# Six edits at the three seams of a two-layer transformer kernel: early routing weights, two moved table loads, one low part on another engine, a residual sum in PSUM

## The chip, the cores and the metric

The kernel runs on one core of a Trainium2 chip. The metric is device time in microseconds (us) of one execution, as the median of several runs. The engines are TensorE (PE, whose weight loads have their own row, PEld), VectorE (DVE), ScalarE (ACT), GpSimd (POOL) and SyncE (SP), which here only issues DMAs. They run their own instruction streams and meet through semaphores.

## The reference

An input of 8 batches x 512 tokens x 128 features passes four sublayers, each followed by a residual sum and a layernorm:

```python
x = layernorm(x + L0_attn(x))   # 16 heads of 8, softmax
x = layernorm(x + L0_ffn(x))    # 32 experts of width 64 (top 6 of 4 groups) + shared expert of width 128
x = layernorm(x + L1_attn(x))   # RMS norm, rotary, sigmoid weights divided by their sum, output projection
x = layernorm(x + L1_ffn(x))    # gated, width 384, integer weights times 1/127
```

The experts are computed densely for all tokens: each expert's hidden values are multiplied by a routing weight per token (zero for most), `combine.T` in the reference's scan, before the down product.

## The kernel before

Four stages follow each other, each a block of its own: `attention0`, `feed_forward` (called "moe" in the tile names), `attention1` and `last_stage` (tiles "ff"). At the end of a block all five engines meet at a barrier and then start the next block's streams. I call the three meeting places seams: seam 1 between `attention0` and `feed_forward`, seam 2 between `feed_forward` and `attention1`, seam 3 between `attention1` and `last_stage`. Features lie on the partitions in the feed-forward stages, and the 512 tokens of a batch are the free dimension.

**Feed-forward units.** The 32 experts are handled two at a time, with the shared expert as the last: 17 units per batch. A unit `j` has three matmuls for the gate (high and low parts of the fp32 numbers, `product`), three for the up product, and three for the down product, which PE does four steps later. ACT applies Silu to the gate in place (L1956), DVE multiplies the up product by the routing weights `cw` (`weighted_up`, L2007) and then by the gate (`weighted_hidden`, L2016), ACT rounds the hidden value to its high part `hh` (`hidden_hi`, L1966), and POOL subtracts to get the low part `hl` (`hidden_lo`, L2077). The third down matmul (L1906) waits for `hl`. PSUM has three banks each for gate and up, so that unit `j + 3` may start when the hidden value of `j` is done. The order on every engine is that of the function `step`, unrolled by hand for the first and last batches.

**Routing weights.** They are computed per batch, written to DRAM as 32 rows (`ct` to `r["weights"]`, for the first batch at L914 in the last part of `attention0`), and read back by SP, each row spread over 64 partitions, into one of eight slots of `cw` (L1862; two DMAs per unit). SP issues all reads of the first batch from the start of the `feed_forward` block.

**The first steps of `feed_forward`** also carry the end of batch 7 of the attention (`FirstOutput`): DVE divides the outputs, POOL adds the residual (L986), DVE takes the statistics, POOL computes the reciprocal root (L178 and L180) and applies the norm (L168, L171).

**The first steps of `last_stage`** carry the end of batch 7 of `attention1` (`LastOutput`, steps `k`). It uses the idle PSUM bank 7, `out_bank(1)`, called `tiles`: PE turns the outputs (k 0, L1579), DVE divides, PE turns them back (k 1, L1584), PE projects (k 2, L1589), DVE adds the bias and the residual (L1616, L1619), takes statistics (k 3), POOL the reciprocal root, DVE applies the norm in four instructions (`layernorm_apply`, L159, k 4), PE turns the result (k 5, L1595), DVE splits it into `xh` and `xl` (L1627, L1629). A unit `s` of this stage has six matmuls (L2156 to L2158 twice) and three down matmuls (L2180, L2181, L2186) three steps later; PE's step `s` calls `last.tensor` with `k = s + 1`, DVE's step `s` with `k = s`. The down product of unit 3 is the first to write bank 7 and waits for `x_parted`, which L1629 raises.

ACT loads a table when the function changes. Three tiny activations place these loads by hand: Silu at the start of `feed_forward` (L1990), Sigmoid at its end (L1993), Silu at the end of `attention1` (L1268).

## Time and profile before

| | |
|---|---|
| median of 3 runs | 1083.58 us (1083.07 to 1086.02) |
| the profiled execution | 1081.41 us, span of its instructions 1079.6 us |
| busy share of the span | PE 93%, DVE 75%, ACT 68%, POOL 43% |
| mean granted TensorE clock | 0.966 of full |
| `feed_forward` block | about 417.3 to 721.5 us |
| `attention1` block | about 721.8 to 1010.0 us |
| `last_stage` block | about 1010.3 to 1079.6 us |

Times inside the trace are us from the span's start. Since PE is busy for nearly all of the span, what matters is where it is idle, or runs at a lower clock, and which engine it then waits for. A matmul's printed duration overlaps the next one's, so a row of matmuls goes by its pitch (start to start), not by the printed durations.

### The profile page before, as it was taken

The page shows a single profiled execution, that of the slowest core. Times are in us where ns is not written, and L with a number is a line of the kernel's source. Part 1 is how long each engine was busy: PE and PEld are TensorE (multiplying, and loading weights), DVE is VectorE, ACT ScalarE, POOL GpSimd, SP SyncE. Part 2 cuts the span into 40 slices and gives each one's busy share as a digit, 9 for nine tenths or more (in the row PEclk, how much of TensorE's full clock was granted, in tenths as well). Part 3 has the DMA queues.
Part 4 walks back from the last instruction along what each step waited for, and adds up shares of the span by engine and source line. Part 5 has one row for each costly group of instructions (what it writes and reads, how often), then busy time and mean ns, then how long its engine had stood idle before and what let it go on. Part 6 is the DMA issues. An engine that isn't in the chain of part 4 may idle for free. (4 is left out here: it accounts for less than half of the span.)

```text
span 1079.6 us, 20047 instructions
## 1 busy us (share of the span) xinstructions
PE 1006.4 (93%) x5764; PEld 475.0 (44%) x5764; DVE 813.6 (75%) x1890; ACT 735.6 (68%) x952; POOL 460.3 (43%) x465
## 2 busy tenths in 40 slices
PE   3999999999999998999999999989999999999796
PEld 1122222222222244888888887753332333222485
DVE  4879999999999975887788789856555555533577
ACT  1057777777777775655555555557888898899554
POOL 0323414224143625676677676665333133300265
PEclk7569999999999999999999999989999999999998
DMA  6363122231221002334323433432522332230011
GB/s 198 108 210 105 56 76 90 62 103 54 85 89 44 2 2 97 114 111 153 116 95 109 146 114 91 155 106 83 152 75 65 94 117 81 65 88 1 1 30 49
DMA packets 74091, 97.00 MB, mean 90 GB/s; under 512 B 12716, under 2 KB 42284, under 8 KB 73644
## 3 DMA queue, kind: packets, MB, share of 16 engines
q1 hardware_dynamic: 73048, 95.17, 28.5%
q10 hardware_dynamic: 992, 1.21, 0.4%
q8 instruction: 25, 0.41, 0.2%
q14 instruction: 26, 0.21, 0.1%
HBM read 68.16 MB, written 27.79 MB: 89 GB/s over the span
## 5 line engine op out<-in xcount | busy, mean ns | idle before, releaser
L687 DVE TENSOR_REDUCE a_nmax<-a_ps_f 128x1 f32<-128x512 f32 x512 | 319.8, 682 | 27.2 <-PE a_ps_f L542 25.8
L470 ACT ACTIVATE a_prob<-a_ps_s 128x1024 f32<-128x1024 f32 x256 | 251.1, 1022 | 74.9 <-PE a_ps_s L607 73.6
L1259 ACT ACTIVATE a_prob<-a_ps_s 128x1024 f32<-128x1024 f32 x256 | 244.8, 1030 | 34.1 <-PE a_ps_s L1314 33.3
L2077 POOL TENSOR_TENSOR moe_hl<-moe_hid,moe_hh 128x512 fp32r<-128x512 f32 x136 | 176.2, 1301 | 90.8 <-ACT moe_hh L1966 90.7
L542 PE MATMUL a_ps_f<-a_ks,a_qs 48*128 48x512 bf16 x512 | 177.1, 415 | 23.9 <-DMA a_ks<-parts_k 10.1
L1956 ACT ACTIVATE moe_ps<-moe_ps 128x512 f32<-128x512 f32 x128 | 74.5, 582 | 111.8 <-PE moe_ps L1886 111.1
L620 PE MATMUL a_ps_o<-a_prob,a_va 128*32 128x512 f32 x1024 | 138.1, 612 | 0.5 <-ACT a_prob L470 0.4
L1327 PE MATMUL a_ps_o<-a_prob,a_va 128*32 128x512 f32 x1024 | 137.2, 608 | 1.0 <-ACT a_prob L1259 0.5
L542 PEld LDWEIGHTS a_ps_f<-a_ks,a_qs 48*128 48x128 bf16 x512 | 40.8, 94 | 218.8 <-DVE a_nmax L687 188.2
L607 PE MATMUL a_ps_s<-a_qs,a_ks 51*128 51x512 bf16 x512 | 135.3, 388 | 1.7 <-ACT a_prob L470 1.5
L2007 DVE TENSOR_TENSOR moe_prod<-moe_cw,moe_ps 128x512 f32<-128x512 f32 x128 | 87.3, 682 | 31.2 <-PE moe_ps L1886 28.3
L1314 PE MATMUL a_ps_s<-a_qs,a_ks 48*128 48x512 bf16 x512 | 92.8, 388 | 12.3 <-ACT a_prob L1259 9.0
L2016 DVE TENSOR_TENSOR moe_hid<-moe_prod,moe_ps 128x512 f32<-128x512 f32 x128 | 86.9, 679 | 6.9 <-DVE moe_prod L2007 1.9
L1966 ACT ACTIVATE moe_hh<-moe_hid 128x512 fp32r<-128x512 f32 x136 | 84.7, 624 | 5.2 <-DVE moe_hid L2016 5.0
L258 POOL TENSOR_TENSOR a_parts<-a_qk,g_zero 128x512 bf16<-128x512 f32 x28 | 29.2, 1044 | 137.3 <-ACT a_qk L442 66.0
L1314 PEld LDWEIGHTS a_ps_s<-a_qs,a_ks 48*128 48x128 bf16 x512 | 23.7, 93 | 133.1 <-ACT a_prob L1259 105.9
L749 POOL TENSOR_TENSOR a_msplit<-a_nmax,g_zero 128x32 bf16<-128x32 f32 x16 | 3.8, 238 | 146.6 <-DVE a_nmax L687 146.6
L1884 PE MATMUL moe_ps<-moe_xh,moe_whig 128*128 (+1 forms) x136 | 55.0, 404 | 3.4 <-DVE moe_hid L2016 3.4
L1906 PE MATMUL moe_ps<-moe_hl,moe_whid 128*128 128x512 f32 x136 | 54.0, 397 | 0.7 <-POOL moe_hl L2077 0.6
L1904 PE MATMUL moe_ps<-moe_hh,moe_wlod 128*128 128x512 f32 x136 | 53.9, 396 | 0.0
L1884 PE MATMUL moe_ps<-moe_xh,moe_whiu 128*128 (+1 forms) x136 | 53.8, 396 | 0.0
L1886 PE MATMUL moe_ps<-moe_xl,moe_whig 128*128 (+1 forms) x136 | 53.6, 394 | 0.0
(294 smaller groups left out, 1590.8 us busy)
## 6 DMA issues: line engine op xcount, KB each, us to landing
moe_cw<-r_weights SPq DMA_DIRECT2D x256, 128.0 KB, 2.9
parts_q<-a_parts SPq DMA_DIRECT2D x48, 256.0 KB, 2.5
a_qs<-parts_q SPq DMA_DIRECT2D x128, 96.0 KB, 2.4
parts_k<-a_parts SPq DMA_DIRECT2D x46, 256.0 KB, 2.5
a_ks<-parts_k SPq DMA_DIRECT2D x121, 96.0 KB, 2.5
a_xt<-in_x_t SPq DMA_DIRECT2D x8, 256.0 KB, 2.9
out_x<-g_X SPq DMA_DIRECT2D x7, 256.0 KB, 2.3
moe_wg<-in_wg SPq DMA_DIRECT2D x1, 1088.0 KB, 6.1
```

Source lines behind the costliest of these rows:

```text
L470: nc.scalar.activation(prob[:, u % PSLOTS, :, :], ps_s[:, u % 2, :, :], ACT.Exp, scale=float(P) ** -0.5).then_inc(exp_done, 1)
L542: nc.tensor.matmul(ps_f[:, bank, :], stack_rows(qs[p], h, QKR)[:, qt * P:(qt + 1) * P], stack_rows(ks[p], h, QKR), start=True, stop=True). ...
L607: mm = nc.tensor.matmul(ps_s[:, u % 2, i, :], stack_rows(ks[p], h, MXR)[:, kt * P:(kt + 1) * P], stack_rows(qs[p], h, MXR), start=True, st ...
L620: mm = nc.tensor.matmul(ps_o[j * CT:(j + 1) * CT, :], v_of_head(va[p], kt, grp * HG + j), prob[:, (2 * e + j // UN) % PSLOTS, j % UN, :], ...
L687: nc.vector.tensor_reduce(nmax[:, half_no, h % 2, col:col + 1], ps_f[:, bank, :], AX.X, ALU.max, negate=True).then_inc(max_done, 1)
L1259: nc.scalar.activation(prob[:, u % PSLOTS, :, :], ps_s[:, u % 2, :, :], ACT.Sigmoid, scale=float(HD) ** -0.5).then_inc(exp_done, 1)
L1314: mm = nc.tensor.matmul(ps_s[:, u % 2, i, :], stack_rows(ks[p], h, QKR)[:, kt * P:(kt + 1) * P], stack_rows(qs[p], h, QKR), start=True, st ...
L1327: mm = nc.tensor.matmul(ps_o[j * CT:(j + 1) * CT, :], v_of_head(va[p], kt, grp * HG + j), prob[:, (2 * e + j // UN) % PSLOTS, j % UN, :], ...
L1884: nc.tensor.matmul(dst, w[0][:, j, :], hi, start=True, stop=False)
L2007: nc.vector.tensor_tensor(prod[:, bank(j), :], cw[:, j % RC, :], ps_u[:, bank(j), :], ALU.mult).then_inc(prod_done, 1)
L2016: nc.vector.tensor_tensor(hid[:, hid_at(j), :], prod[:, bank(j), :], ps_g[:, bank(j), :], ALU.mult).then_inc(hid_done, 1)
L2077: nc.gpsimd.tensor_tensor(hl[:, part_at(j), :], hid[:, hid_at(j), :], hh[:, part_at(j), :], ALU.subtract).then_inc(hl_done, 1)
```

## The change

- **Routing weights requested earlier.** SP, at the end of its `attention0` stream, waits until the first batch's weights are in DRAM and issues the reads of units 0 to 2 (`CW_EARLY = 3`, six DMAs) there. `cw` moves to the top of the free SBUF, and slots are renumbered (`cw_slot`), so that these three units use the top three slots. In `feed_forward` SP starts with unit 3.
- **Sigmoid load moved** from after ACT's last instruction of `feed_forward` to right behind the last `hidden_hi`.
- **Silu load moved** from the end of `attention1` to the start of `last_stage`.
- **Last low part on VectorE.** For unit 16 of batch 7 DVE computes `hl` in `feed_forward`, not POOL.
- **Residual sum in PSUM.** In `LastOutput` the sum of L1619 is written to `tiles` (PSUM) and not back to `att` (SBUF), and the statistics and the four norm instructions read it there.
- **Turn later.** PE's turn of the normed tile and DVE's split of it come at k 6, not at k 5.

```diff
+RC, CW_EARLY = 8, 3
...
         sp.dma_start(self.m["r"]["weights"][0:E, :], self.m["ct"][:, :]).then_inc(self.m["c_out"], 16)
+        sp.wait_ge(self.m["c_out"], 16)
+        for j in range(CW_EARLY):
+            read_weights(sp, self.m, 2 * j, j)
...
+def cw_slot(j):
+    return (j + RC - CW_EARLY) % RC
+
+def read_weights(sp, m, row, j):
+    for i in range(2):
+        src = m["r"]["weights"][bass.ds(row + i, 1), :].broadcast_to([EI, T])
+        sp.dma_start(m["cw"][i * EI:(i + 1) * EI, cw_slot(j), :], src).then_inc(m["cw_in"][j % RC], 16)
...
             take_o(NB - 1, NO - 1)
-            nc.scalar.activation(e["table"][:, :], g["zero"][:, :], ACT.Silu)
...
-        if k == 5:
+        if k == 6:
             pe.wait_ge(self.ln["x_done"], NB)
             pe.wait_ge(self.y_taken, NB + 1)
...
-            nc.vector.tensor_tensor(att[:, :, :], att[:, :, :], self.X, ALU.add).then_inc(self.sum_done, 1)
+            nc.vector.tensor_tensor(tiles, att[:, :, :], self.X, ALU.add).then_inc(self.sum_done, 1)
         if k == 3:
             dve.wait_ge(self.sum_done, NB)
-            layernorm_stats(nc, dve, ln, NB - 1, att)
+            layernorm_stats(nc, dve, ln, NB - 1, tiles)
         if k == 4:
-            layernorm_apply(nc, dve, g, ln, NB - 1, att)
-        if k == 5:
+            layernorm_apply(nc, dve, g, ln, NB - 1, tiles)
+        if k == 6:
             dve.wait_ge(self.x_turned, NB)
...
                 def batch(b, more):
-                    for j in range(n_c):
+                    for j in range(CW_EARLY if isinstance(b, int) and b == 0 else 0, n_c):
                         load_weights(b, j)
...
-                pe.wait_ge(hl_done, n + 1 + C)
+                if isinstance(b, int) and (b, j) == (NB - 1, n_un - 1):
+                    pe.wait_ge(last_low, 1)
+                else:
+                    pe.wait_ge(hl_done, n + 1 + C)
...
                     hidden_hi(*at(b, j, HI))
+                    if head and is_last_unit(b, j):
+                        nc.scalar.activation(head.e["table"][:, :], g["zero"][:, :], ACT.Sigmoid)
...
-            if head:
-                nc.scalar.activation(head.e["table"][:, :], g["zero"][:, :], ACT.Sigmoid)
...
+                if is_last_unit(b, j):
+                    dve.wait_ge(hh_done, n_un * NB + C)
+                    nc.vector.tensor_tensor(hl[:, part_at(n_un - 1), :], hid[:, hid_at(n_un - 1), :],
+                                            hh[:, part_at(n_un - 1), :], ALU.subtract).then_inc(last_low, 1)
...
-                if at(b, j, HI) is not None:
+                if at(b, j, HI) is not None and not is_last_unit(b, j):
                     hidden_lo(*at(b, j, HI))
...
+            nc.scalar.activation(last.table[:, :], g["zero"][:, :], ACT.Silu)
             for s in steps:
                 if batch_at(s, END) is not None:
                     take_down(batch_at(s, END))
...
+            m["cw"] = nc.alloc_sbuf_tensor_at("moe_cw", [P, RC, T], F32, offset=wide - RC * T * 4)
+            m["cw_in"] = [sem(f"cw_in{i}") for i in range(RC)]
```

## Rows read from the trace of the kernel before

**Rows 1.** Windows: stretch, length, busy PE, PEld, DVE, ACT, POOL, then PEclk, DMA.
```profile
1024.00:1026.00 2.00, 2.00 (x7) 1.52 (x6) 1.38 (x2) 0.00 (x0) 0.00 (x0) 0.50 0.00 0
...
1030.00:1040.00 10.00, 10.00 (x47) 8.21 (x46) 7.55 (x29) 5.32 (x10) 7.33 (x9) 1.00 0.09 26
```

**Rows 2.** Timeline around seam 1: start, us, engine, line, tiles, idle before.
```profile
411.78 0.33 SPq L914 DMA_DIRECT2D r_weights<-moe_ct  x1
...
416.41 0.60 ACT L442 ACTIVATE moe_dsb<-a_ps_o 128x512 f32<-128x512 f32 x1 [0.52 <-PE a_ps_o L620]
417.29 10.81 SPq L1862 DMA_DIRECT2D moe_cw<-r_weights  x17
...
417.47 0.63 PE L928 MATMUL moe_ps<-g_ident,moe_dsb 128*128 128x128 f32 x4 [1.19 <-PEq L290]
...
421.29 0.69 DVE L2007 TENSOR_TENSOR moe_prod<-moe_cw,moe_ps 128x512 f32<-128x512 f32 x1 [2.17 <-DMA moe_cw<-r_weights]
...
422.79 0.63 ACT L1966 ACTIVATE moe_hh<-moe_hid 128x512 fp32r<-128x512 f32 x1 [0.62 <-DVE moe_hid L2016]
...
425.44 0.20 POOL L178 TENSOR_TENSOR a_ve<-a_mv,g_eps 128x4 f32<-128x4 f32 x1 [0.24 <-DVE a_mv L150]
...
430.29 0.19 PEld L1906 LDWEIGHTS moe_ps<-moe_hl,moe_whid 128*128 128x128 f32 x1 [0.53 <-POOL moe_hl L2077]
```

**Rows 3.** The DMA of L914, from issue to landing (source view).
```profile
DMA to landing us min/median/max: 1.6/1.6/1.6
```

**Rows 4.** Timeline around seam 2.
```profile
714.31 1.73 ACT L1966 ACTIVATE moe_hh<-moe_hid 128x512 fp32r<-128x512 f32 x3
...
715.01 3.78 POOL L2077 TENSOR_TENSOR moe_hl<-moe_hid,moe_hh 128x512 fp32r<-128x512 f32 x3 [0.78 <-ACT moe_hh L1966]
...
718.17 0.40 PE L1904 MATMUL moe_ps<-moe_hh,moe_wlod 128*128 128x512 f32 x1
...
720.00 1.28 ACT L1993 ACT_TABLE_LOAD   x1
...
720.80 0.69 DVE L2050 TENSOR_TENSOR moe_y<-moe_ps,g_X 128x512 f32<-128x512 f32 x1 [5.42 <-PE moe_ps L1916]
```

**Rows 5.** Timeline a little later: a VectorE sum beside a GpSimd one.
```profile
729.34 1.04 POOL L168 TENSOR_TENSOR moe_y<-moe_y,moe_mv 128x512 f32<-128x512 f32 x1
729.41 1.52 DVE L1416 TENSOR_TENSOR a_xr<-a_xb,a_rr 128x512 f32<-128x512 f32 x1 [1.12 <-POOL a_rr L1533]
```

**Rows 6.** Timeline around seam 3.
```profile
1007.90 0.60 ACT L1247 ACTIVATE a_osb<-a_ps_o 128x512 f32<-128x512 f32 x1 [1.25 <-PE a_ps_o L1327]
1008.52 1.28 ACT L1268 ACT_TABLE_LOAD   x1
...
1010.31 0.63 PE L1579 MATMUL ff_ps<-g_ident,a_osb 128*128 128x128 f32 x4 [2.53 <-PEq L1183]
...
1011.67 0.60 ACT L2215 ACTIVATE ff_gated<-ff_ps 128x512 f32<-128x512 f32 x1 [1.66 <-PE ff_ps L2158]
...
1012.44 0.69 DVE L2244 TENSOR_TENSOR ff_hid<-ff_gated,ff_ps 128x512 f32<-128x512 f32 x1 [0.36 <-PE ff_ps L2158]
```

**Rows 7.** Timeline of the norm of batch 7 in the last stage.
```profile
1019.77 2.49 POOL L2287 TENSOR_TENSOR ff_hl<-ff_hid,ff_hh 128x512 fp32r<-128x512 f32 x2
1019.84 3.02 DVE L159 TENSOR_SCALAR g_X<-a_att,a_mv,a_rstd 128x128 f32<-128x128 f32 x4 [0.83 <-POOL a_rstd L180]
...
1022.91 1.11 PE L1595 MATMUL ff_ps<-g_ident,g_X 128*128 128x128 f32 x4 [3.04 <-DVE g_X L159]
...
1029.39 0.47 PE L2180 MATMUL ff_ps<-ff_hh,ff_whid 128*128 128x512 f32 x1
```

**Rows 8.** Timeline: POOL's row, then DVE's, of the next norm in that stage.
```profile
1033.27 2.55 POOL L2287 TENSOR_TENSOR ff_hl<-ff_hid,ff_hh 128x512 fp32r<-128x512 f32 x2
...
1033.33 1.36 DVE L159 TENSOR_SCALAR g_X<-ff_ps,ff_mv,ff_rstd 128x128 f32<-128x128 f32 x4 [0.83 <-POOL ff_rstd L180]
```

**Rows 9.** The chain that ended last, at full clock: start, us to the next step.
```profile
1026.42 0.23 PE ff_ps L2156
...
1029.20 0.44 PE ff_ps L2193 x4
```

More of the change, by code:

```diff
@@ L1557, in attention1 @@
     return LastOutput(nc, g, w[:, 3, :], ob, osb[:, NO - 1, :], rec, att, att_t, ln, xh[:, NB - 1, :], xl[:, NB - 1, :],
-                      ot_done, rec_done, att_done, at_done, at_taken, y_done, y_taken, sum_done, x_turned, x_hi, x_parted)
+                      ot_done, rec_done, att_done, at_done, at_taken, y_done, y_taken, sum_done, x_turned, x_hi, x_parted,
+                      e["table"])
 class LastOutput:
     def __init__(self, nc, g, w, ob, osb, rec, att, att_t, ln, xh, xl, ot_done, rec_done, att_done, at_done, at_taken,
-                 y_done, y_taken, sum_done, x_turned, x_hi, x_parted):
+                 y_done, y_taken, sum_done, x_turned, x_hi, x_parted, table):
         self.nc, self.g, self.w, self.ob, self.osb, self.rec, self.att, self.att_t, self.ln = (
@@ L1570, in __init__ @@
             y_done, y_taken, sum_done, x_turned, x_hi, x_parted)
-        self.X = g["X"][:, NB - 1, :, :]
+        self.X, self.table = g["X"][:, NB - 1, :, :], table
     def tensor(self, pe, ps, k):
@@ L1764, in feed_forward @@
         RG = 3
-        RC = 8
         RH = min(4, n_un)
@@ L1780, in feed_forward @@
             ct = m["ct"]
-            cw = sb("cw", [P, RC, T])
+            cw, slot = m["cw"], cw_slot
             ps_ct = ps[0:E, 7, :]
-            c_out, cw_in = m["c_out"], [sem(f"cw_in{i}") for i in range(RC)]
+            c_out, cw_in = m["c_out"], m["cw_in"]
         g_done, u_done, silu_done, prod_done, hid_done, hh_done, hl_done, d_done, d_taken = (
@@ L1787, in feed_forward @@
         t_done, t_taken, ct_turned, ct_taken = sem("t_done"), sem("t_taken"), m["ct_turned"], m["ct_taken"]
+        last_low = sem("last_low")
         C = 6
@@ L1836, in head_at, with is_last_unit @@
             return n_un * (b - NB + 2) + j if head and isinstance(b, int) and b >= NB - 2 else None
+        def is_last_unit(b, j):
+            return isinstance(b, int) and at(b, j, HI) == (NB - 1, n_un - 1)
         def routes(b):
@@ L1859, in load_weights @@
                         sp.wait_ge(prod_done, n_un * (b - 1) + j + n_c - RC + 1 + C)
-                    for i in range(2):
-                        src = r["weights"][bass.ds(b * E + 2 * j + i, 1), :].broadcast_to([EI, T])
-                        sp.dma_start(cw[i * EI:(i + 1) * EI, j % RC, :], src).then_inc(cw_in[j % RC], 16)
+                    read_weights(sp, m, b * E + 2 * j, j)
                 def batch(b, more):
-                    for j in range(n_c):
+                    for j in range(CW_EARLY if isinstance(b, int) and b == 0 else 0, n_c):
                         load_weights(b, j)
@@ L2006, in weighted_up @@
                 dve.wait_ge(cw_in[j % RC], 32 * (n_c // RC) * b + 32 * (j // RC) + 32)
-                nc.vector.tensor_tensor(prod[:, bank(j), :], cw[:, j % RC, :], ps_u[:, bank(j), :],
+                nc.vector.tensor_tensor(prod[:, bank(j), :], cw[:, slot(j), :], ps_u[:, bank(j), :],
                                         ALU.mult).then_inc(prod_done, 1)
```

## The prediction, made before the change was run

> **What bounds the kernel now.** I read the page first: PE is busy 93% of the span, and on the chain that ended last nearly all time is PE's. So a change is worth what it takes out of PE's idle time, or out of its time at a low clock, and nothing else. The windows of the last stage show the two conditions [rows 1]: from 1030 to 1040 us PE is busy all 10 us at full clock (2.4 GHz) with DVE at 7.55 and POOL at 7.33, so there PE is the bound and an earlier start is kept to the end. From 1024 to 1026 the granted clock is 0.50 (1.2 GHz). A step of the 512-column matmuls takes 0.23 us at full clock and four turns take 0.44 [rows 9]. Then I read the timeline at the three seams and at the norm of batch 7 in the last stage, asking at each what PE waits for last. The sum is made against the profiled execution (1081.41 us, span 1079.6). The median of the runs lies 2.2 us above it, which I take as the spread of executions, so I subtract the same gain from the median.
>
> **Seam 1, early routing weights.** ACT ends the attention at 416.41 + 0.60 = 417.01 and SP's first issue of the next block is at 417.29, so the barrier costs 0.28 [rows 2]. DVE then waits 2.17 us for the first weights and starts its product at 421.29. The up product was there long before: PE starts at 417.47, and four turns (0.44) and six matmuls (1.37) with the last one's tail end by 419.5 [rows 2, 9]. What is removed is that wait. What is added is six issues on SP in front of the barrier. The first block's issues go at 10.81 / 17 = 0.636 us each. The DRAM write is issued at 411.78 and lands 1.6 us later [rows 3], so SP issues from about 413.4 and ends at 413.45 + 6 x 0.636 = 417.27. That is 0.26 after ACT: SP becomes the last at the barrier, and everybody starts 0.26 later, which costs 0.26. The DMAs themselves collide with nothing: no transfer of the attention is open then. The slots are requested from unit 3 on as before, and are needed later than before by nobody.
>
> DVE's chain gets shorter by 421.29 - 419.5 - 0.26 = 1.5, of which I lose some 0.2 to GpSimd's residual sum running beside DVE's next instruction. But PE does not get the 1.3 us. It idles three times at the start of this stage, and the last time it waits for POOL, at 430.29 [rows 2]. POOL's chain up to there starts with the first `hh`, which ACT could have begun at 422.79 - 0.62 = 422.17 (it idled 0.62 for the hidden value). In the new kernel ACT begins it as soon as it is free, at 422.17 + 0.26 = 422.43, so 0.36 earlier than before. POOL's own work follows without a gap, and its idle 0.24 before L178 goes too, since the statistics come 1.3 earlier. POOL's chain therefore gains 0.36 + 0.24 = 0.60, and PE with it. Behind 430.29 PE has no idle time worth naming. Seam 1: **-0.6**. Bounds: nothing, if POOL's work stretches by as much, to -1.3, if POOL's chain moves with DVE's.
>
> **Seam 2, low part on DVE and Sigmoid.** The last `hh` ends at 714.31 + 1.73 = 716.04, and POOL does the last three low parts one after the other until 715.01 + 3.78 = 718.79 [rows 4]. PE could have begun its last matmul one step after the one at 718.17, at 718.40; it begins at 718.85. So 0.45 us is there to gain if DVE's subtraction is ready by 718.40. DVE asks for it at about 716.1, when POOL is inside its first subtraction. Two sums over SBUF beside each other can be seen a little later [rows 5]: DVE's took 1.52 and not the 0.69 of its like in [rows 4]; it asked at 729.41, POOL's ended at 730.38, and it was done at 730.93. It waited, and then went ahead of POOL's next. If it does so here, it runs from about 716.2 to 716.9 and POOL's second subtraction ends at about 718.05, not 717.53. PE's third matmul of unit 15 waits for that, and unit 16's comes 0.80 behind (three steps and the release), at about 718.9: no gain. If POOL goes first, DVE ends at 718.2, still in time, and 0.45 is gained. I take **0**, with -0.45 and +0.3 as bounds, because in [rows 5] the one that had waited went first.
>
> The Trainium skill ("SBUF — State Buffer", section Who interferes with whom) has this as a rule: a VectorE instruction with two SBUF inputs and a GpSimd one that reads SBUF exclude each other for the whole instruction. By that rule the edit as such gains nothing or 0.45 as order decides; [rows 5] agree with it.
>
> The Sigmoid load lies at 720.00 on ACT and ends with its activation at 721.49. Moved behind the last `hh` it runs from 716.04 to 717.5, inside ACT's idle time before 719.38, so it costs nothing. It gains nothing either: DVE's sum at 720.80 + 0.69 = 721.49 ends at the same moment and holds the barrier. Without the cover it would cost what it costs now.
>
> **Seam 3, Silu.** ACT takes the last outputs until 1008.50, loads the table for 1.28 from 1008.52, runs its activation (0.2, to 1010.01), and PE starts 0.30 later, at 1010.31 [rows 6]. Without load and activation ACT is at the barrier 1.51 earlier. At seam 1, where ACT's last work was such a take right behind PE's, PE's first instruction came 417.47 - 417.01 = 0.46 behind it and not 0.30 [rows 2], so I count 1.51 - 0.16 = 1.35. ACT itself starts its load at the same moment as PE, at 1008.50 + 0.46, and is done at 1008.96 + 1.28 + 0.2 = 1010.44; the first Silu is wanted at 1011.67 - 1.35 = 1010.32. It ends at 1011.1, when DVE wants it (1012.44 - 1.35 = 1011.09). Hidden to within 0.05. Seam 3: **-1.35**, between -1.1 and -1.5.
>
> The Trainium skill ("ScalarE: Activation LUTs", What ACT_TABLE_LOAD costs) adds about 1.38 us of drain to each load. Here the activation follows 0.01 us behind the load, so the rows show none; by the page the gain would be larger.
>
> **The norm in the last stage.** DVE's four norm instructions, asked for at 1019.84, took 3.02 us while POOL did two subtractions until 1022.26 [rows 7]. The same four took 1.36 one batch later, with their input in PSUM and POOL again at two subtractions from 1033.27 [rows 8]. So it is the SBUF input that makes DVE wait for POOL; with PSUM, the norm ends at 1019.84 + 1.36 = 1021.2. The statistics read PSUM from now on; I count no cost for that, and the turn's 0.57 of slack below would cover one. Now PE: its last matmul before the turn ends at 1019.87, of which 0.16 is overlap, so it is free at 1019.71 and idles until 1022.91. With k 6 it goes on with three down matmuls (0.69) and unit 5 (six, 1.37), and comes to the turn at 1021.77, 0.57 behind the norm: no wait. Then the turn 0.44, down 0.69, unit 6 1.37, turn of batch 0 0.44, and the down matmul of unit 3 at 1019.71 + 5.0 = 1024.71, against 1029.39 before [rows 7]. `x_parted` must be there: the turn ends at 1022.4, DVE is done with unit 5's hidden value at 1022.65, and two instructions of 0.69 end at 1024.05. It holds with 0.65 to spare. The gain is **-4.68**: 3.20 of idle time, and 1.48 because the ten matmuls and turns behind it ran at half clock [rows 1]. PSUM alone at k 5 would have left an idle 1.5. Bounds: if the clock falls all the same, 3.2 remain; if the norm from PSUM waits for POOL as the other did (ends 1022.86), PE idles 1.1 at the turn, and 3.6 remain, or about 2.2 with the low clock.
>
> **Sum.** 0.6 + 0 + 1.35 + 4.68 = 6.6 us. 1083.58 - 6.6 = **1077.0**; in the profiled execution 1074.8.
>
> **Rivals.**
> 1. *The stall at the norm only shrinks* (low clock or wait stays, above): 6.6 less 1.1 to 2.5, so 1078.1 to 1079.5. For it: POOL's subtractions lie at the same place. Against: [rows 8]. Chance 0.14.
> 2. *More than the sum*: POOL's chain at seam 1 follows DVE's and seam 2 gives 0.45, or the half clock that follows seam 2 stays away: 1 to 3 us more, 1074.0 to 1076.0. Against: PE's sparse stretch from 716 to 722.4 stays as long. Chance 0.15.
> 3. *SP holds seam 1.* Each us that SP is late costs all engines one. With issues of 1.2 us (twice the row) SP ends at 420.7, 3.4 late, and the total gain is 3.2: 1080.4, no measurable change. It decides against the change, slower by 0.3%, when SP is about 10 us late, issues of 2.2 us. Nothing in the rows has that. 0.05 for the first, 0.01 for the second.
> 4. *The clock falls in the last stage and stays*, the case on the other side: each matmul at half clock costs 0.23 more. From 1019.7 on a low stretch of 43 matmuls would eat the gain, and one of some 57 makes the kernel slower than 1086.8. For it: it did fall once in this stage, behind 3 us of idle time. Against: that idle time is what is removed, and it lasted some ten matmuls. Chance 0.03.
> 5. *The gain is given back*: a later wait in the last stage or the spread of executions hides half of it, 1080.4 to 1083. Against: PE at 10.00 of 10 [rows 1]. Chance 0.05.
>
> The forecast has 0.57, with a range of its own of 1075.8 to 1078.2. The measurement can tell about 0.3%, 3.25 us, so below 1080.3 is faster: 0.88; same 0.08; slower 0.04. The range for 8 in 10 takes in rivals 1 and 2: 1074.2 to 1080.0.
>
> **What would show it.** Seam 1: six issues of L1862's successor end near 417.3, the barrier opens at about 417.55, DVE's first product at 419.8, and PE's wait for POOL at 429.7. Seam 2: DVE's subtraction lasts longer than 0.69 or POOL's second does. Seam 3: PE's first turn 0.43 behind the take. The norm: four instructions in 1.36, no idle time on PE before the turn, clock 1.00 throughout. The prediction is wrong if PE's idle time moves to the down matmul of unit 3 (`x_parted` late), or if SP is last at the barrier by more than 1 us.

## The result, and the profile after

The changed kernel takes 1075.41 us as the median of 5 runs (1074.43 to 1077.16), beside 1083.07 us for the kernel before (5 runs, 1081.81 to 1086.02). The ratio is 0.9921, with a 95% interval from 0.9906 to 0.9937: faster, by 7.7 us in the medians. In the profiled executions the span goes from 1079.6 to 1073.2 us, which is 6.4 us, and the mean granted clock from 0.966 to 0.968. One execution of the kernel before, run beside the experiments below, took 1229.53 us at a mean granted clock of 0.763; it was in a slower state of the chip and no comparison uses it.

The kernel after has other line numbers (L914 is L915, L1862 is L1177, L2077 is L2102, L1595 is L1611, L2180 is L2205). The page's first two parts:

```profile
span 1073.2 us, 20047 instructions
## 1 busy us (share of the span) xinstructions
PE 1003.9 (94%) x5764; PEld 473.8 (44%) x5764; DVE 814.2 (76%) x1891; ACT 735.5 (69%) x952; POOL 459.8 (43%) x464
...
PEclk7579999999999999999999999999999999999999
```

The page hardly shows the change: PE's share goes from 93% to 94%. The timeline shows it. **Seam 1** after, to be held against [rows 2]; first the timeline of SP alone, then that of all engines:

```profile
411.99 0.33 SPq L915 DMA_DIRECT2D r_weights<-moe_ct  x1
413.61 3.77 SPq L1177 DMA_DIRECT2D moe_cw<-r_weights  x6
```

The other engines at the same place:

```profile
416.63 0.60 ACT L443 ACTIVATE moe_dsb<-a_ps_o 128x512 f32<-128x512 f32 x1 [0.52 <-PE a_ps_o L621]
418.23 0.63 PE L932 MATMUL moe_ps<-g_ident,moe_dsb 128*128 128x128 f32 x4 [1.73 <-PEq L291]
...
420.28 0.69 DVE L2028 TENSOR_TENSOR moe_prod<-moe_cw,moe_ps 128x512 f32<-128x512 f32 x1 [0.40 <-PE moe_ps L1904]
...
422.82 0.62 ACT L1987 ACTIVATE moe_hh<-moe_hid 128x512 fp32r<-128x512 f32 x1
...
425.17 0.21 POOL L179 TENSOR_TENSOR a_ve<-a_mv,g_eps 128x4 f32<-128x4 f32 x1
...
430.01 0.19 PEld L1927 LDWEIGHTS moe_ps<-moe_hl,moe_whid 128*128 128x128 f32 x1 [1.08 <-POOL moe_hl L2102]
```

All distances below are counted from ACT's last take (416.63; before 416.41), because the attention ends 0.22 later in this execution. SP's six issues end at 413.61 + 3.77 = 417.38, and PE starts at 418.23, 0.85 behind them. From the take to PE's first turn there are 1.60 us now and were 1.06. DVE's first product waits for PE and no longer for a DMA, and comes 3.65 behind the take instead of 4.88. PE's last wait there, the one for POOL (L1927 at 430.01), ends 13.38 behind it instead of 13.88.

**Seam 2** after, beside [rows 4]:

```profile
714.10 1.73 ACT L1987 ACTIVATE moe_hh<-moe_hid 128x512 fp32r<-128x512 f32 x3
...
714.80 2.98 POOL L2102 TENSOR_TENSOR moe_hl<-moe_hid,moe_hh 128x512 fp32r<-128x512 f32 x2 [0.79 <-ACT moe_hh L1987]
...
715.87 0.78 DVE L2067 TENSOR_TENSOR moe_hl<-moe_hid,moe_hh 128x512 fp32r<-128x512 f32 x1 [0.70 <-ACT moe_hh L1987]
...
717.83 0.50 PE L1927 MATMUL moe_ps<-moe_hl,moe_whid 128*128 128x512 f32 x1 [0.72 <-POOL moe_hl L2102]
...
718.64 0.39 PE L1927 MATMUL moe_ps<-moe_hl,moe_whid 128*128 128x512 f32 x1
```

DVE takes 0.78 us and POOL's two take 2.98, where two without a DVE subtraction beside them take 2.52 (POOL at 428.68 in the same trace). PE's last matmul waits for nothing, but it stands behind unit 15's, which waited for POOL: the last copy starts 4.97 behind the start of the three `hh` and was 5.07 behind.

**Seam 3** after, beside [rows 6]:

```profile
1007.57 0.60 ACT L1263 ACTIVATE a_osb<-a_ps_o 128x512 f32<-128x512 f32 x1 [1.25 <-PE a_ps_o L1342]
1008.44 1.28 ACT L2254 ACT_TABLE_LOAD   x1 [0.27 <-PEq L1199]
1008.48 0.63 PE L1595 MATMUL ff_ps<-g_ident,a_osb 128*128 128x128 f32 x4 [1.03 <-PEq L1199]
...
1009.74 0.20 ACT L2254 ACTIVATE a_table<-g_zero 128x1 f32<-128x1 f32 x1
...
1009.85 0.60 ACT L2240 ACTIVATE ff_gated<-ff_ps 128x512 f32<-128x512 f32 x1
```

From the take's start to PE there are 0.91 us; before there were 2.41. **The norm of batch 7** after, beside [rows 7]:

```profile
1017.98 2.55 POOL L2313 TENSOR_TENSOR ff_hl<-ff_hid,ff_hh 128x512 fp32r<-128x512 f32 x2
1018.05 1.37 DVE L160 TENSOR_SCALAR g_X<-ff_ps,a_mv,a_rstd 128x128 f32<-128x128 f32 x4 [0.84 <-POOL a_rstd L181]
...
1019.97 0.60 PE L1611 MATMUL ff_ps<-g_ident,g_X 128*128 128x128 f32 x4
...
1021.55 0.69 DVE L1645 TENSOR_TENSOR ff_xl<-ff_ps,ff_xh 128x512 fp32r<-128x512 f32 x1
...
1022.82 0.48 PE L2205 MATMUL ff_ps<-ff_hh,ff_whid 128*128 128x512 f32 x1
```

The windows view of that stretch, with the columns of [rows 1]:

```profile
1018.00:1020.00 2.00, 2.00 (x11) 1.57 (x10) 1.95 (x5) 1.05 (x3) 2.00 (x3) 1.00 0.00 0
```

The four norm instructions take 1.37 us beside the same two subtractions of POOL. PE has no idle time in front of the turn and keeps the full clock. From PE's first turn of the stage to the down matmul of unit 3 there are 1022.82 - 1008.48 = 14.34 us, and there were 19.08.

The pieces add up to the span's difference: 0.43 from the take to the three `hh` (of which 0.50 at seam 1, 0.07 given back on the way), 0.10 at seam 2, 0.01 at its barrier, 1.50 at seam 3 and 4.74 at the norm are 6.78. The later take costs 0.22 and the tail behind unit 3 is 0.17 longer (50.38 against 50.21): 6.39 of 6.4.

### The profile page after: what moved, and what is told of

Read it like the earlier page. It is cut to its first block and busy times, and to the rows that moved or that the text cites. A ratio compares the mean times of both kernels' runs of the same rounds, so it can differ in the third digit from the quotient of the medians.

```text
span 1073.2 us, 20047 instructions
## 1 busy us (share of the span) xinstructions
PE 1003.9 (94%) x5764; PEld 473.8 (44%) x5764; DVE 814.2 (76%) x1891; ACT 735.5 (69%) x952; POOL 459.8 (43%) x464
## 5 line engine op out<-in xcount | busy, mean ns | idle before, releaser
L471 ACT ACTIVATE a_prob<-a_ps_s 128x1024 f32<-128x1024 f32 x256 | 251.2, 1022 | 74.8 <-PE a_ps_s L608 73.5
L2102 POOL TENSOR_TENSOR moe_hl<-moe_hid,moe_hh 128x512 fp32r<-128x512 f32 x135 | 175.5, 1305 | 90.0 <-ACT moe_hh L1987 89.9
L1927 PE MATMUL moe_ps<-moe_hl,moe_whid 128*128 128x512 f32 x136 | 53.9, 396 | 1.4 <-POOL moe_hl L2102 1.4
L1903 PE MATMUL moe_ps<-moe_xh,moe_wlog 128*128 (+1 forms) x136 | 53.6, 394 | 0.0
```

The costliest lines, as they stand in the source:

```text
L471: nc.scalar.activation(prob[:, u % PSLOTS, :, :], ps_s[:, u % 2, :, :], ACT.Exp, scale=float(P) ** -0.5).then_inc(exp_done, 1)
L2102: nc.gpsimd.tensor_tensor(hl[:, part_at(j), :], hid[:, hid_at(j), :], hh[:, part_at(j), :], ALU.subtract).then_inc(hl_done, 1)
```

## The experiments

All are edits of the changed kernel. Single executions of one kernel lie up to 8 us apart (the kernel before on one chip: 1080.42 to 1088.22), so the local distances decide, and the medians stand beside them. Where a ratio has an interval, it overlaps that of the changed kernel (0.9906 to 0.9937) for all but the last kernel, so no other median tells a variant from it. Each was measured on one chip together with runs of the kernel before. The columns: when ACT's last take of `attention0` begins; from the take at seam 1 to PE's first turn, to DVE's first product, to the end of PE's wait for POOL, and to the three `hh` of batch 7; from these to the last copy of `feed_forward`; at seam 3 from the take to PE; from there to unit 3's down matmul; the span.

| kernel | take | PE | product | wait end | `hh` | copy | seam 3 | unit 3 | span |
|---|---|---|---|---|---|---|---|---|---|
| before | 416.41 | 1.06 | 4.88 | 13.88 | 297.90 | 5.07 | 2.41 | 19.08 | 1079.6 |
| after | 416.63 | 1.60 | 3.65 | 13.38 | 297.47 | 4.97 | 0.91 | 14.34 | 1073.2 |
| no early requests | 419.91 | 1.06 | 5.20 | 14.18 | 299.79 | 4.97 | 0.91 | 14.34 | 1078.8 |
| two early units | 415.28 | 1.06 | 3.11 | 12.86 | 298.44 | 4.97 | 0.91 | 14.34 | 1072.6 |
| three more DMAs | 415.99 | 3.51 | 6.34 | 16.90 | 300.94 | 4.96 | 0.90 | 14.32 | 1075.9 |
| last low part on POOL | 416.54 | 1.61 | 3.66 | 13.38 | 297.40 | 5.06 | 0.91 | 14.33 | 1073.2 |
| three low parts on DVE | 415.52 | 1.62 | 3.68 | 13.41 | 297.46 | 3.70 | 0.91 | 14.34 | 1070.3 |
| Sigmoid load back | 417.25 | 1.61 | 5.21 | 14.94 | 300.61 | 4.97 | 0.90 | 14.34 | 1076.8 |
| Silu load back | 416.33 | 1.61 | 5.22 | 14.98 | 300.68 | 4.96 | 2.41 | 17.04 | 1080.3 |
| turn at k 5 | 416.39 | 1.61 | 5.17 | 15.01 | 300.66 | 4.97 | 0.90 | 16.00 | 1078.9 |
| norm from SBUF | 416.01 | 1.61 | 3.67 | 13.41 | 297.47 | 4.95 | 0.91 | 15.59 | 1074.0 |
| the same, POOL held | 417.52 | 1.61 | 5.18 | 14.93 | 300.43 | 4.96 | 0.91 | 14.31 | 1078.2 |
| combined | 416.87 | 1.06 | 3.11 | 12.86 | 296.92 | 3.72 | 0.91 | 14.36 | 1071.1 |
| combined, PE filled | 416.62 | 1.06 | 3.11 | 12.85 | 296.87 | 3.71 | 0.90 | 14.36 | 1070.5 |

The takes differ though no edit lies before them: the sixteenth `exp` of `attention0` already begins between 81.5 and 83.6 us in thirteen of the profiles, and this difference stays to the end. In the fourteenth, without early requests, it begins at 86.2, behind a half clock from 79 to 86 us that the others don't have. So some 3.3 us of that kernel's span have nothing to do with its edit, and spans must not be compared without the takes.

**Seam 1: how many early requests.** Three kernels: none, two units, and three units with three more DMAs behind them that nothing reads (`cw_copy` is a scratch tensor in DRAM).

```diff
-RC, CW_EARLY = 8, 3
+RC, CW_EARLY = 8, 2          # two early units
...
+        for i in range(3):    # three more DMAs
+            sp.dma_start(self.m["copy"][i, :, :], self.m["r"]["weights"][bass.ds(i, 1), :].broadcast_to([EI, T])).then_inc(self.m["copied"], 16)
```

> The changed kernel without early requests: all weights are requested in the second block. Mine, that the early requests were worth only what GpSimd's chain allowed, less the late barrier (0.49 together by the two traces): DVE waits 2.2 us for the first weights again, PE's wait for GpSimd's low part ends about 0.45 later than in the changed kernel, span 1073.65. Rival, that PE gets what DVE's chain loses: 1.0 to 1.5 us, span 1074.2 to 1074.7.

> The changed kernel with two units' weights requested early, four issues and not six. Mine, that SP was last at the barrier of seam 1: its issues end at 416.2, the barrier opens with ACT again (PE's first turn 0.46 behind the end of ACT's take, not 1.0), every later event of seam 1 comes 0.54 earlier because GpSimd's chain starts with the stage, and the span falls to 1072.7. Rival, that the opening does not matter because PE waits for something bound elsewhere, or that the third unit's weights are now late: span 1073.2 or more, with a DMA wait before DVE's third product.

> The changed kernel with three further DMAs of 128 KB (the routing rows spread into a DRAM scratch that nobody reads) issued by SP behind the six early ones. From the start of ACT's last take in the first attention to PE's first turn of the next block it is 1.06 us before, 1.60 changed, 1.06 with four issues. Mine, that each issue on SP in front of the barrier holds all engines: 3 x 0.64 more, 3.5 us, and GpSimd's low part and the end come 1.9 later too. Rival, that the opening is held by something else than SP's issues: 1.6.

Without early requests the median is 1077.13 us, ratio 0.9928 (0.9901 to 0.9955). PE is back at 1.06, DVE waits for the DMA again (2.48 us, where the kernel before waited 2.17), and PE's wait for POOL ends 0.80 later than with the change. Expected were 0.45; the first weights landed 0.31 later here than in the kernel before, and that is most of the difference. It stays below the 1.0 to 1.5 of the rival. With two units the median is 1075.89, ratio 0.9917 (0.9888 to 0.9945). The barrier opens as early as in the kernel before, DVE does not wait for the weights, and all of 0.52 us comes on top at the wait for POOL. With three more DMAs (one execution, 1077.66 us) PE starts 3.51 behind the take, as expected and as the timeline shows:

```profile
415.99 0.60 ACT L443 ACTIVATE moe_dsb<-a_ps_o 128x512 f32<-128x512 f32 x1 [0.52 <-PE a_ps_o L621]
416.79 1.86 SPq L920 DMA_DIRECT2D cw_copy<-r_weights  x3
...
419.50 0.63 PE L934 MATMUL moe_ps<-g_ident,moe_dsb 128*128 128x128 f32 x4 [3.65 <-PEq L291]
```

SP ends at 418.65 and PE starts 0.85 later, the same distance as with six issues. So SP holds the barrier in the changed kernel, and each issue behind the six costs everybody its 0.62 to 0.63 us. The wait for POOL ends 3.52 later than with the change, not 1.9: the barrier accounts for 1.91, and the clock fell at 420 (below). The third unit is one too many: with two early units none of DVE's first six products waits for a DMA.

**Seam 2: who subtracts.**

```diff
# last low part on POOL
-                if isinstance(b, int) and (b, j) == (NB - 1, n_un - 1):
-                    pe.wait_ge(last_low, 1)
...
-                if at(b, j, HI) is not None and not is_last_unit(b, j):
+                if at(b, j, HI) is not None:
# three low parts on DVE
-                    dve.wait_ge(hh_done, n_un * NB + C)
-                    nc.vector.tensor_tensor(hl[:, part_at(n_un - 1), :], hid[:, hid_at(n_un - 1), :],
+                    for q in range(n_un - 3, n_un):
+                        dve.wait_ge(hh_done, n_un * (NB - 1) + q + 1 + C)
+                        nc.vector.tensor_tensor(hl[:, part_at(q), :], hid[:, hid_at(q), :],
```

> The changed kernel with the last low part back on GpSimd. Mine, that the port made DVE's subtraction and POOL's exclude each other, so that the edit gained nothing at seam 2: the third down matmul of unit 16 comes 2.4 to 2.6 us behind that of unit 14, as it does in the changed kernel (2.49), POOL does three subtractions in 3.78 us, and the span stays at 1073.2 within 0.15. Rival, that the edit was worth its 0.45 and something else took it back: 2.9 us between the two matmuls and a span of 1073.65.

> The changed kernel with the low parts of units 14, 15 and 16 of batch 7 all on VectorE, so that GpSimd reads no SBUF there. Mine: with no GpSimd sum beside them the three subtractions take 0.69 each, from 715.1 to about 717.2, the third down matmul of unit 16 comes 1.4 us behind that of unit 14 and not 2.49, and the span falls by 1.1 us to 1072.1. Rival, that POOL's speed or the port is not what sets this place: the matmuls stay 2.4 us apart and the span stays at 1073.2.

With the last part back on POOL, unit 14's to unit 16's last matmul is 718.47 - 715.99 = 2.48 us, against 2.49 after; the last copy is 0.09 later, and the span is the same 1073.2; the median is 1077.58, ratio 0.9935 (0.9913 to 0.9957). With all three on DVE it is 1.40, PE doesn't wait, and the copy comes 1.27 earlier; the span falls by more (1070.3), of which 1.11 is the earlier take. The median is 1076.25, ratio 0.9919 (0.9895 to 0.9942). Its timeline:

```profile
713.97 0.69 DVE L2069 TENSOR_TENSOR moe_hl<-moe_hid,moe_hh 128x512 fp32r<-128x512 f32 x1
...
714.57 1.29 DVE L2069 TENSOR_TENSOR moe_hl<-moe_hid,moe_hh 128x512 fp32r<-128x512 f32 x2
...
714.85 0.40 PE L1928 MATMUL moe_ps<-moe_hl,moe_whid 128*128 128x512 f32 x1
...
715.55 0.39 PE L1928 MATMUL moe_ps<-moe_hl,moe_whid 128*128 128x512 f32 x1
...
716.25 0.40 PE L1928 MATMUL moe_ps<-moe_hl,moe_whid 128*128 128x512 f32 x1
```

DVE needs 0.69 us for what takes POOL 1.26 to 1.29, but one part on DVE beside two on POOL gives the time back, because POOL's second then takes 1.69. With POOL out of it the speed counts. Two parts on DVE and one on POOL were not tried.

**The two table loads, each put back where it was.**

```diff
-                    if head and is_last_unit(b, j):
-                        nc.scalar.activation(head.e["table"][:, :], g["zero"][:, :], ACT.Sigmoid)
...
+            if head:              # Sigmoid load back
+                nc.scalar.activation(head.e["table"][:, :], g["zero"][:, :], ACT.Sigmoid)
...
             take_o(NB - 1, NO - 1)
+            nc.scalar.activation(e["table"][:, :], g["zero"][:, :], ACT.Silu)   # Silu load back
```

> The changed kernel with the Sigmoid load back at the end of ACT's stream of the second stage. Mine, that DVE's sum holds that barrier anyway: from the start of ACT's last copy (the down product of batch 7) to SP's first issue of the next block 2.4 us, as in both kernels (2.39 before, 2.38 changed). Rival, that the load is on the path: 0.3 or more longer.

> The changed kernel with the Silu load back in front of the barrier of seam 3. From the start of ACT's last take to PE's first turn of the last stage it is 2.41 us before and 0.91 changed. Mine: 2.4 again, all 1.5 us of it on the end, span 1.5 longer, the rest of the stage as changed (distance 14.34). Rival, that the load only moves the wait from the barrier to the first Silu: the rest of the stage gets shorter by part of it, distance under 14.0.

The Sigmoid load at its old place changes nothing at seam 2: from the last copy to SP's first issue behind the barrier there are 2.38 us with either. One execution, 1078.63 us. The Silu load at its old place costs exactly the 1.50 at seam 3 (2.41 against 0.91). The median is 1079.97, ratio 0.9949 (0.9931 to 0.9967). It costs 2.70 more up to unit 3, which was not expected: see the clock, below.

**The norm: two remedies, one at a time.**

```diff
-        if k == 6:
+        if k == 5:            # turn at k 5, twice (PE and DVE)
...
-            nc.vector.tensor_tensor(tiles, att[:, :, :], self.X, ALU.add).then_inc(self.sum_done, 1)
+            nc.vector.tensor_tensor(att[:, :, :], att[:, :, :], self.X, ALU.add).then_inc(self.sum_done, 1)  # norm from SBUF
...
                 last.gpsimd(pool, s)
+                if s == 3:    # POOL held, with the norm from SBUF
+                    pool.wait_ge(last.ln["x_done"], NB)
```

> The changed kernel with the turn back at step 5, PSUM kept. Distances are from PE's first turn in the last stage to the first down matmul of unit 3: 19.08 us before, 14.34 changed. Mine: the norm still lasts 1.37, PE reaches the turn before it ends and idles 1.5 us, no fall of the clock: distance 15.9, of the 4.74 gained 3.2 stay. Rival, that the later turn does nothing and PSUM is all: 14.3. Rival, that an idle time of this place brings the clock down whatever its length: over 17.

> The changed kernel with the sum, the statistics and the norm in SBUF as before, the turn at step 6. Mine: the four norm instructions last 3.0 us again, each waiting for a GpSimd subtraction; PE has 2.1 us of other work meanwhile and idles 1.1 at the turn; distance 15.4, clock 1.00. Rival, that the place of the sum does not matter once the turn is late: 14.3.

> As the kernel with the sum in SBUF and the turn at step 6, but GpSimd starts its two subtractions only when the norm is done. If it is GpSimd's reading of SBUF beside it that stretched the norm, the four instructions last 1.1 us as in the attention stages, though their input is in SBUF, PE does not wait at the turn, and the distance is 14.3 to 14.5. If an SBUF input is slow by itself here, they last 3.0 us again and the distance is 15.4 or more.

PSUM alone (the turn at k 5) leaves PE idle for 1.41 us and brings unit 3 to 16.00 (15.9 was expected), with no fall of the clock behind it; the later turn alone (norm from SBUF) leaves 1.02 idle and gives 15.59. The medians are 1077.07, ratio 0.9922 (0.9905 to 0.9939), and 1076.03, ratio 0.9929 (0.9905 to 0.9953). Both together give 14.34. The timeline's row of the norm from SBUF beside POOL:

```profile
1017.54 3.06 DVE L160 TENSOR_SCALAR g_X<-a_att,a_mv,a_rstd 128x128 f32<-128x128 f32 x4 [0.83 <-POOL a_rstd L181]
```

And with POOL held, its subtractions behind it:

```profile
1023.09 1.12 DVE L160 TENSOR_SCALAR g_X<-a_att,a_mv,a_rstd 128x128 f32<-128x128 f32 x4 [0.83 <-POOL a_rstd L181]
...
1024.29 2.55 POOL L2313 TENSOR_TENSOR ff_hl<-ff_hid,ff_hh 128x512 fp32r<-128x512 f32 x2 [1.24 <-DVE g_X L160]
```

So the 3.06 us are not the price of SBUF: alone the four instructions take 1.12 us there, less than the 1.37 from PSUM. They are a wait for POOL. Holding POOL until the norm is done gives 14.31 to unit 3, the same as PSUM; one execution, 1080.02 us.

The Trainium skill has this as a rule ("SBUF — State Buffer", Who interferes with whom): a scalar-operand instruction of VectorE can enter a mode with two ports, and then it and GpSimd block each other for the whole instruction. These two rows agree with it.

**Combined.** Two early units and three low parts on DVE.

> The version that the experiments point to: two units' weights early, not three, and the low parts of units 14 to 16 on VectorE. Mine: 0.53 from seam 1 and 1.3 to 1.5 from seam 2 against the changed kernel, 1.9 us together, so about 9 us against the kernel before (ratio 0.992 less 0.0018, 0.990). Rival, that the two gains don't add: no better than the kernel with the three low parts alone.

The median is 1074.04 us (6 runs, 1071.87 to 1076.57), ratio 0.9912 (0.9885 to 0.9938), beside 1084.37 for the kernel before on that chip (ten runs). Both local gains are there in full, the wait's end at 12.86 and the copy at 3.72, so the two add. That the span (1071.1) is above that of the three low parts alone (1070.3) comes from the take, which is 1.35 later.

**The clock.** The largest miss of the expectations above is one thing: in several kernels `hh` comes some 3 us late though the edit lies elsewhere. The granted clock in windows of 2 us explains it. The table sums, over the windows from 416 to 1060, 2 us times what the clock lacks of 1.00; so 1.70 is a stretch of 3.4 us at 0.50 (1.2 GHz). The windows' two decimals leave each figure open by 0.02.

| kernel | stretches below full clock: where, and what the clock lacks (us) | sum |
|---|---|---|
| before | 722-730: 3.42; 1022-1028: 1.70 | 5.1 |
| after; last low part on POOL | 720-730: 3.42; 720-728: 3.42 | 3.4 |
| no early requests; two early units | 682-688 / 676-682: 1.72; 726-736 / 720-730: 3.40 | 5.1 |
| three more DMAs | 420-424: 1.70; 724-732: 3.40 | 5.1 |
| three low parts on DVE; combined | 720-724 / 720-726: 1.70 | 1.7 |
| norm from SBUF | 746-752: 1.70 | 1.7 |
| Sigmoid load back | 418-424: 1.70; 680-686: 1.72; 724-730: 1.70 | 5.1 |
| turn at k 5; POOL held | 418-424: 1.70 / 1.72; 680-686: 1.72 / 1.70; 724-730 / 726-730: 1.70 / 1.72; 752-758: 1.70 | 6.8 |
| Silu load back | 416-422: 1.70; 680-686: 1.70; 724-730: 1.70; 1010-1020: 3.42 | 8.5 |
| combined, PE filled | none | 0 |

The windows at seam 1 with the turn at k 5, whose edit lies 600 us later:

```profile
415.00:417.00 2.00, 1.07 (x8) 0.16 (x8) 0.00 (x0) 1.47 (x3) 0.00 (x0) 1.00 0.58 201
417.00:419.00 2.00, 1.00 (x5) 1.03 (x6) 0.00 (x1) 0.98 (x1) 0.00 (x0) 0.79 0.67 183
419.00:421.00 2.00, 2.00 (x6) 1.52 (x6) 0.84 (x3) 1.09 (x3) 1.04 (x1) 0.50 0.65 186
421.00:423.00 2.00, 2.00 (x9) 1.64 (x8) 1.44 (x3) 0.58 (x1) 0.23 (x1) 0.86 0.60 204
```

PE had worked for 1.07 of 2 us, stood idle for 1.74, and had just started again (at 418.00) when the clock fell, at 418.15; its first matmuls then went at 0.43 us each instead of 0.23, DVE waited 1.68 us for them, and `hh` came 3.2 later for two such stretches that lack 3.42 together. The second one, at 681, follows idle times of PE as well: 1.63 and 0.67 us, from 677.32 and 679.61. The same two idle times stand in the changed kernel, where the clock did not fall, and with two early units, where it did; in all it fell there in six of the fourteen profiles. Of the eight kernels with 1.7 us of idle time there, four fell and four did not, and the one with 3.65 fell. Of the five with 1.2 (take to PE 1.06) none did. With the Silu load back the clock fell at seam 3 behind 2.5 us of idle time, and unit 3 came 2.70 later for a lack of 3.42; the kernel before had the same idle time there and no fall.

Does PE's idle time bring this about? In the last kernel PE gets nine matmuls that nobody reads in front of seam 2's barrier, on top of the combined kernel (they only add work):

```diff
             def turn(b):
 
+                last = routed and isinstance(b, int) and b == NB - 1
+                if last:
+                    product(ps_g[:, bank(n_un), :], wg, (xh[:, b, :], xl[:, b, :]), 2)
                 pe.wait_ge(d_taken, b + 1 + C)
...
                 mm.then_inc(t_done, 1)
+                if last:
+                    for i in range(2):
+                        product(ps_g[:, bank(n_un), :], wg, (xh[:, b, :], xl[:, b, :]), i)
```

> This is the combined kernel (two early units at seam 1, low parts of units 14 to 16 on DVE) with nine further matmuls on PE into a PSUM bank that is no longer read: three in PE's idle 0.69 us before its turn of the last batch of feed_forward, and six behind the turn, in the 1.7 us before seam 2's barrier. Their result is used by nobody. In the combined kernel's profile PE is busy 0.66 of the 2 us from 718 to 720 and idle to 720.54, and the granted clock is 0.64 in 721 to 722 and 0.50 in 722 to 724. A low-clock stretch that begins between 720 and 726 stands in eleven of the twelve other kernels' profiles with the change (in the twelfth one comes at 746). Theory 1, PE's idle time in front of the barrier brings the clock down: no window from 718 to 730 is below 1.00, a stretch may come later (as in the one at 746) or not at all, the exp of attention1 to its last take is 283.9 to 284.4 us, and the span is 1070.3 to 1071.1 in otherwise like conditions, 0 to 0.5 us better. Theory 2, the fall has nothing to do with this idle time (it follows from the mixed start of attention1): the same 0.50 windows at about 721 to 724 stand, and the span is unchanged. Both: the fillers end at about 718.9 + 1.4 = 720.2 and delay the barrier by nothing, or by up to 0.2.

The windows at seam 2 with the fillers, columns as in [rows 1]:

```profile
716.00:718.00 2.00, 2.00 (x9) 1.30 (x9) 0.37 (x1) 1.33 (x3) 0.00 (x0) 1.00 0.00 0
718.00:720.00 2.00, 1.91 (x10) 1.29 (x9) 0.69 (x1) 0.00 (x0) 0.00 (x0) 1.00 0.00 0
720.00:721.00 1.00, 0.20 (x2) 0.14 (x4) 0.14 (x1) 0.00 (x0) 0.84 (x1) 1.00 0.00 0
721.00:722.00 1.00, 1.00 (x10) 0.66 (x6) 0.96 (x8) 0.77 (x1) 1.00 (x4) 1.00 0.75 189
722.00:723.00 1.00, 0.82 (x7) 0.40 (x5) 0.54 (x4) 1.00 (x2) 1.00 (x3) 1.00 0.93 307
```

The clock stays at 1.00 from the start through seam 2 and until 1065, behind PE's last matmul (1063). That speaks for the idle time as the cause. The other executions, of which only the mean granted clock is known, agree: all four with the fillers have 0.998, and none of the combined kernel's six is above 0.996, which is what its profile with one such stretch has. It is not proof: one of the twelve others (norm from SBUF) kept its clock at this place too; the fillers also open the barrier later, and that this shift and not PE's work kept the clock was not excluded; and all four executions also lack the half clock from about 10 to 72 us, which four of the combined kernel's six have and which an edit at seam 2, 650 us later, does not explain.

The stretch from the first `exp` of `attention1` to its last take shrinks from 284.39 to 283.67, more than expected. The barrier opens 0.57 later than in the combined kernel (2.96 against 2.39 from copy to SP), where at most 0.2 was expected: PE's last filler ends at 719.51 + 0.40 = 719.91, and SP follows 0.25 behind it. I had measured the room up to PE's next start, which lies 0.64 behind the barrier's opening in both kernels (720.80 - 720.16; 720.54 - 719.90), and not up to the opening. So from the last copy of `feed_forward` to the last take of `attention1` only 0.15 us is gained (287.85 to 287.70), and of the 0.6 by which the span (1070.5) is shorter 0.25 is the earlier take. The median is 1072.19 us, ratio 0.9883 (0.9867 to 0.9900), and its four runs lie between 1071.69 and 1072.47, where the combined kernel's six lie between 1071.87 and 1076.57. This is the fastest version that was run. That the scatter of the others comes from stretches like these fits the mean clocks on record: of the kernel before, eleven of the eighteen executions on one chip lack the early half clock, and their spans go from 1078.6 at 0.992 over 1083.5 to 1084.3 at 0.990 to 1086.3 at 0.987. Where the lack sits is known only for the profiled ones.

## Why the prediction was right

The forecast was 1077.0 us, range 1074.2 to 1080.0; the median is 1075.4. The gain in the profiled execution was forecast at 6.6 us (1074.8) and is 6.4 (1074.96). That is nearer than the median, which gained 7.7; the other 1.1 lies within what executions scatter and has no step of the prediction behind it. Some of the agreement is luck: both profiled executions have the early half clock and the same 3.4 us lacking behind seam 2, while profiles of kernels with the same code up to there differ by 3 us of `hh` from the clock alone. Step by step:

**Seam 1: forecast -0.6, measured -0.50.** The mechanism held: SP is the last at the barrier, and PE's gain is set by POOL's chain and not by DVE's wait of 2.17 [rows 2]. Two sizes were off. SP's issues were sized well (3.77 / 6 = 0.628 against 0.636), but they hold the barrier for 0.54 and not 0.26: PE starts 0.85 behind SP's last issue, while it started 0.46 behind ACT's last work, and I had charged SP with ACT's distance. And the first `hh` came 0.19 earlier, not 0.36; the rest of POOL's chain gave 0.31, where 0.24 was counted. What the forecast did not see is that two units would do: they keep the gain without the loss and are worth 1.02 against the kernel before.

**Seam 2: forecast 0, measured -0.10.** The choice between the bounds was right. DVE's subtraction, asked for while POOL was in its first, went ahead of POOL's second, which then took 2.98 - 1.29 = 1.69 us. With the part back on POOL the last copy moves by 0.09. The Sigmoid load is worth nothing in either place, as forecast, since DVE's sum holds the barrier.

**Seam 3: forecast -1.35, measured -1.50.** PE starts 0.31 behind ACT's take (1008.48 - 1008.17), so the distance is the 0.30 of [rows 6] and not the 0.46 of seam 1 that I deducted. The first Silu was hidden, as forecast: table and activation end at 1009.94, and the first gate starts with them. The drain of 1.38 us of the Trainium skill's page ("ScalarE: Activation LUTs", What ACT_TABLE_LOAD costs) is not seen: the gain is the load's 1.28 and the activation's 0.2.

**The norm: forecast -4.68, measured -4.74.** Every step came as told: 1.37 for the four instructions (1.36), 0.55 between their end and the turn (0.57), `x_parted` 0.58 ahead of unit 3 (0.65). "PSUM alone at k 5 would have left an idle 1.5" was 1.41. The experiments confirm the cause that rows of before could only suggest, that DVE waits for POOL, by taking POOL away instead of SBUF. The 1.48 for the half clock was gained in this execution, but it is the one term that is not certain. The fall at this place stands in one profile only, that of the kernel before, and the table shows that at the other seams like idle times go with a fall in some executions and without one in others.

**The rivals.** The stall did not shrink, it went. "More than the sum" did not come in the span. The median is inside that rival's band (1074.0 to 1076.0) and just outside the forecast's own (1075.8 to 1078.2), but none of its three ways happened: POOL's chain did not follow DVE's, seam 2 gave 0.10 and not 0.45, and the half clock behind seam 2 stayed. SP does hold seam 1, at a price of 0.54 and not 3.4. The clock did fall at seam 3 in one kernel (Silu load back), so rival 4's mechanism exists, at 2.70 us. The counts given for that rival were too high: at 0.23 us each, 29 half-clock matmuls eat the 6.6 us and 43 (9.9 us) make the kernel slower, not 43 and 57. Nothing was given back later in the last stage: the tail behind unit 3 is 0.17 longer.

## What to carry to other kernels

When an engine that only issues DMAs gets work in front of a barrier, count each issue (0.63 us here) and its own distance to the next block's first matmul (0.85 us behind SP's last issue, 0.31 to 0.46 behind ACT's last work), and move only as many transfers as the first consumers need. When two engines wait for each other over SBUF, moving one of three like instructions to the faster engine gave 0.1 us here and moving all three 1.3; moving one side's operand to PSUM removed the wait as well. And when a distant edit seems to cost microseconds, look at the granted clock around each sparse stretch of PE before explaining the median.

## What was not expected of the hardware

- The clock falls to 0.50 at the same seams in some profiles and not in others, behind 1.7 us of idle time on PE at seam 1 (four of eight), behind 1.63 and 0.67 us near 680 (six of fourteen), and once behind 2.5 us at seam 3. Each fall in the table lacks 1.70 to 1.72 or 3.40 to 3.42 us. In `feed_forward` nearly all of it is paid (3.2 us of `hh` for 3.42; 1.5 for 1.72 with two early units); behind seam 2 less is (from the last copy to the last take of `attention1` 288.51 us with 3.42 lacking, 287.85 with 1.70 in the combined kernel).
- Seven of the fourteen profiles also hold a half clock from about 10 to 72 us that lacks 29 to 31 us. It costs next to nothing: the attention's last take is at 416.63 with it (the changed kernel) and at 416.62 without it (combined, PE filled). With either clock DVE is busy 19.6 of the 20 us from 40 to 60 and PE 18.9 to 19.0. A half clock a little later is paid: in the kernel without early requests it lacks 3.4 us from 79 to 86, and the sixteenth `exp` comes 3.5 us later than with the last low part on POOL, whose clock is full there.
- A GpSimd subtraction that meets a VectorE one took 1.69 us instead of 1.26 to 1.29, while the VectorE one took 0.78 instead of 0.69.
